# Cross-attention and routed FFN on one core: token list by two 128-column matmuls and a mask, down pieces a gap further up, third tile's logits by halves, first expert's pieces rearranged

## The chip, the core and the metric
The kernel runs on one core of a Trainium2 chip. A core has TensorE (PE), VectorE (DVE), ScalarE (ACT), GpSimd (POOL) and SyncE (SP), each with its own instruction queue, and they meet through semaphores. The metric is the device time of one execution in microseconds (us), as a median of several runs. The kernel before took 310.98 us (median of 3 runs, 310.86 to 312.36).

## The reference, cut to what matters
```python
# x: (2,1024,256)  ctx: (2,64,256)  16 heads of 64
def xattn(q_in, kv):                       # q_in = layernorm(x)
    q = einsum('bqc,chd->bqhd', q_in, Wq) / 8;  k, v = kv @ Wk, kv @ Wv
    a = einsum('bqhd,bkhd->bhqk', q, k)
    a = softmax(einsum('bhqk,hi->biqk', a, Wth1))      # heads mixed before
    a = einsum('bhqk,hi->biqk', a, Wth2)               # ... and after
    return einsum('bqhd,hdc->bqc', einsum('bhqk,bkhd->bqhd', a, v), Wo)
x = x + xattn(layernorm(x), ctx)
f = layernorm(x).reshape(2048, 256)
scores = (layer_norm(f) * g + b) @ centroids.T         # (2048, 8)
taken = all False
for e in range(8):                                     # balanced: 256 tokens each
    idx_e = top_k(where(taken, -inf, scores[:, e]), 256); taken[idx_e] = True
for e in range(8):
    h = layer_norm(f[idx_e]) * g + b
    out[idx_e] = f[idx_e] + gelu(h @ w1[e] + b1[e]) @ w2[e] + b2[e]
x = x + out
```

## The kernel before
**Attention.** The 2048 tokens are 16 tiles of 128. The head mixing is folded into two factors per batch: Am, which makes a tile's 1024 logits (16 heads by 64 keys) from its 256 columns of x, and Bm, which makes the tile's output from its 1024 probabilities. The tiles run through steps: in step s, tile s gets its logits, tile s-1 its exponential (ACT) and sums (DVE), tile s-2 is transposed on PE and multiplied with Bm, tile s-3 has its residual and layer norm, tile s-4 its scores and its row, which is stored to memory for the gathers of the experts. PE's function `attn` is in this order: first the 8 transposes of tile s-2, then 12 logits matmuls of tile s. An operand of a product in fp32r comes in two parts, a rounded one and a rest, and a product takes three matmuls (rounded with rounded, rounded with rest, rest with rounded, `mm3`). The statistics of x (`x_stats`, 16 tiles, `x_variance`, and POOL's `x_root`) are made by DVE early, tiles 8 to 15 in its loop over the factors' pieces.

**Routing.** For each of the 8 experts, DVE and PE find the 256th largest score by a search of 8 rounds of 4 bits. A round is `compare` (DVE, `cmpb` L1018), `total(k,r)` (PE, `oh_b,cntb`), the turn (DVE, `ok` L1035 and three small ones) and `narrow` (L1052). `select` and `ranks` follow: DVE makes `GE` and the running sums `INC`, PE multiplies them (`GE,tri_b` and `INC,ones_b`), and from this DVE gets each token's rank, marks the tokens as taken in `M`, and PE writes the next expert's scores with them (`cst,M`, `spread_scores`).

**Token list.** From each token's slot DVE makes one-hot tiles of its low and high half, `Loh` and `Hoh` (16 tiles by 16), POOL makes `Htk` = Hoh times token number, PE's `tokens` adds 16 products of 16 by 16 in PSUM, ACT's `lists_out` copies it to `Rt`, PE's `spread` multiplies with `exp_r` to spread it over 128 partitions, and DVE's `indices` picks by a mask and adds (`Rx`, `idx`). `idx` drives POOL's gather of the rows `G`.

**Experts.** An expert's rows are transposed (PE `cst,G`), scaled by ACT into `yF` (plain) and `yT` (rounded part), and POOL's `y_rest` makes the rest of yT. `up(e,f)`, f = 0..7, is six matmuls `yT,w1p` of 256 columns; ACT makes the gelu `hT`; `down(e,n)`, n = 0..15, is one fp32 matmul `w2s,hT`, two records in the trace. The last two experts have their down part as fp32r (`w2p,hp`), for which DVE's `hidden_split` makes two parts (`hp`, L1140 and L1142). DVE's `final` (L1059) adds the down result to the rows and POOL scatters them to the output.

**Order.** Slot k searches for expert k, makes the list of expert u = k-1, and does the up rest and the down part of expert e = k-2. Where PE's pieces stand is set by tables: `UP_FIRST`, `UP_REST`, `UP_LATE` and `DOWN` give, for each gap, which pieces run there; gap r is ahead of total(k,r), gap 8 between the last total and `ranks`, gap 9 behind `ranks`. All engines work through their queues in order. Through slot 1 there is no expert work ready, and PE runs products of `ones_b` (`keep_busy`) as padding. `lists_out` of expert 7's list and its `tokens` stand at the end of slot 7.

## Time and profile before
| what | value |
| --- | --- |
| median of 3 runs | 310.98 us (310.86 to 312.36) |
| profiled execution | 311.05 us |
| its span, first to last instruction | 309.3 us |
| granted TensorE clock, mean | 0.991 |
| busy: PE, DVE, ACT, POOL | 94%, 74%, 49%, 64% |
| instructions | 6795 |

The profiled execution took 1.75 us beyond its span. The stretches of the kernel in that trace: 0 to 50 us loads and factors, with the first logits; 50 to 164 the tiles, 7.14 us each (from the second to the third period: 72.09, 79.23, 86.37); 164 to 184 the search of slots 0 and 1, a round in 1.19 us; 184 to 297 the slots 2 to 8, the full ones in 15.3 us each; then the end of the last expert. In the rows below, a line of a timeline is the start in us, the duration in us, the engine, line, operation and tiles, with how many instructions it joins (x6), and in brackets the idle time of the engine just before and what ended it.

### The profile page before, as it was taken

To read this page: it belongs to the slowest core of one execution; us is meant where nothing else is said; L and a number is where in the kernel's file an instruction comes from. 1 tells how busy PE (TensorE), PEld (TensorE's weight loads), DVE (VectorE), ACT (ScalarE), POOL (GpSimd) and SP (SyncE) were. 2 spreads that over 40 slices of the span, in tenths; PEclk is the share of its full clock that TensorE was granted. 3 is DMA by queue.
4 is the path that set the end of the run, shared out by engine and by line. 5 is a ranking of instruction groups with operands and counts; after the bars stand their busy time and mean duration, and the time that the engine had idled before them with its cause. 6 is when DMAs were issued, how large, how long until landed. Compare 5 with 4: busy or idle time off the path is not lost.

```text
span 309.3 us, 6795 instructions
## 1 busy us (share of the span) xinstructions
PE 291.3 (94%) x2151; PEld 252.6 (82%) x2151; DVE 229.2 (74%) x799; ACT 151.0 (49%) x275; POOL 198.8 (64%) x248
## 2 busy tenths in 40 slices
PE   7999998999999999999987779999999999999990
PEld 3989997999999999999982239797989898989980
DVE  0569999888887888888877877777777777338750
ACT  1257646355555555554546424544444454564720
POOL 8200333467888888877742785949787878768841
PEclk9999999999999999999999999999999999999996
DMA  7995002971000000000116420555656565712120
GB/s 254 359 368 207 3 0 76 368 271 35 36 34 34 34 34 34 34 34 35 37 67 206 135 70 2 157 187 166 214 170 208 175 206 174 222 37 69 36 74 28
DMA packets 21769, 37.79 MB, mean 122 GB/s; under 512 B 2416, under 2 KB 14960, under 8 KB 21360
## 3 DMA queue, kind: packets, MB, share of 16 engines
q1 hardware_dynamic: 19184, 31.16, 29.4%
q0 software_dynamic: 2560, 6.31, 6.7%
q8 instruction: 14, 0.23, 0.3%
q14 instruction: 11, 0.09, 0.1%
HBM read 31.17 MB, written 6.29 MB: 121 GB/s over the span
## 4 chain that ended last, share of the span: by engine, by line
PE 77%; DVE 11%; issue 3%; POOL 3%; DMA 2%; ACT 1%; POOLq 0%; DVEq 0%
PE pair L1208 68%; PE pair L1284 4%; PE pair L1258 2%; DVE cmpb L1018 2%; PE pair L1452 1%; PE pair L1296 1%; DMA G<-rows_scratch,idx 1%; DMA out_dram<-G,idx 1%; DVE sm L875 1%; DVE wneg L789 1%; DVE pair L1052 1%; DVE hp L1140 1%; POOL out_dram L543 1%; DVE ok L1035 1%; POOL pr L284 0%
## 5 line engine op out<-in xcount | busy, mean ns | idle before, releaser
L1208 PE MATMUL pair<-yT,w1p 128*128 128x256 f32 x384 | 53.3, 290 | 0.0
L1208 PE MATMUL pair<-Bm,pT 128*128 (+1 forms) x384 | 50.4, 287 | 0.2 <-ACT pT L630 0.2
L1208 PEld LDWEIGHTS pair<-yT,w1p 128*128 128x128 f32 x384 | 48.2, 191 | 0.5 <-POOL yT L528 0.2
L1208 PE MATMUL pair<-Am,xTp 128*128 (+1 forms) x192 | 48.3, 400 | 0.0
L1208 PEld LDWEIGHTS pair<-Bm,pT 128*128 128x128 f32 x384 | 47.1, 191 | 0.4 <-issue 0.4
L1208 PE MATMUL pair<-w2s,hT 128*128 128x256 f32 x192 | 47.1, 389 | 0.0
L284 POOL TENSOR_TENSOR pr<-pr,rs 128x1024 f32<-128x1024 f32 (+1 forms) x16 | 31.3, 1955 | 24.3 <-DVE rs L882 15.2
L522 POOL TENSOR_TENSOR w1p<-w1s,w1p 128x512 fp32r<-128x512 f32 x32 | 40.1, 1280 | 5.7 <-ACT w1p L696 5.6
L1208 PEld LDWEIGHTS pair<-Am,xTp 128*128 128x128 f32 x192 | 34.9, 188 | 6.9
L1208 PEld LDWEIGHTS pair<-w2s,hT 128*128 128x128 f32 x192 | 33.8, 190 | 4.3
L741 ACT ACTIVATE hT<-pair,b1s 128x256 f32<-128x256 f32 x48 | 20.2, 471 | 34.4 <-PE pair L1208 20.9
L465 POOL TENSOR_TENSOR xTp<-xTs,xTp 128x256 fp32r<-128x256 f32 x16 | 11.9, 743 | 29.5 <-ACT xTp L597 29.5
L625 ACT ACTIVATE pr<-pr,r 128x1024 f32<-128x1024 f32 x16 | 18.4, 1149 | 25.2 <-DVE pr L927 25.2
L512 POOL DMA_INDIRECT G<-rows_scratch,idx x16 | 15.8, 987 | 17.3 <-DVE idx L1122 14.9
L1018 DVE TENSOR_SCALAR_CACHE_REDUCE cmpb<-pair 128x256 bf16<-128x256 f32 x48 | 23.5, 489 | 1.9
L923 DVE TENSOR_REDUCE mx<-pair 128x16 f32<-128x1024 f32 x16 | 19.5, 1221 | 4.1 <-PE pair L1208 3.9
L888 DVE TENSOR_TENSOR pT<-pair,pT 128x512 fp32r<-128x512 f32 x32 | 21.3, 668 | 0.3 <-ACT pT L630 0.3
L1208 PE MATMUL pair<-ones_b 128*128 128x512 bf16 x66 | 19.9, 424 | 1.5 <-DVE ones_b L778 1.5
L543 POOL DMA_INDIRECT out_dram<-G,idx x16 | 15.9, 992 | 7.7 <-DVE G L1059 3.1
L927 DVE TENSOR_TENSOR pr<-pair,mx 128x1024 f32<-128x1024 f32 x16 | 19.6, 1225 | 1.5
L1035 DVE SCALAR_TENSOR_TENSOR ok<-pair,cst 128x16 f32<-128x16 f32 x54 | 9.3, 173 | 13.8 <-PE pair L1208 13.7
L875 DVE TENSOR_REDUCE sm<-pr 128x16 f32<-128x1024 f32 x16 | 19.3, 1204 | 0.1
(156 smaller groups left out, 573.6 us busy)
## 6 DMA issues: line engine op xcount, KB each, us to landing
w1s<-w_dram SPq DMA_DIRECT2D x8, 1024.0 KB
w2s<-w_dram SPq DMA_DIRECT2D x7, 1024.0 KB, 5.8
rows_scratch<-row SPq DMA_DIRECT2D x16, 256.0 KB, 2.0
xs<-x_dram SPq DMA_DIRECT2D x1, 2048.0 KB, 16.7
xTs<-xT_dram SPq DMA_DIRECT2D x1, 2048.0 KB, 18.4
wk_s<-wk_dram SPq DMA_DIRECT2D x1, 1024.0 KB, 5.5
wv_s<-wv_dram SPq DMA_DIRECT2D x1, 1024.0 KB, 7.6
wqT_s<-wqT_dram SPq DMA_DIRECT2D x2, 512.0 KB, 9.2
```

The lines of the kernel that those rows point to most:

```text
L284: return eng.tensor_tensor(p4, p4, rs[:, v, :].unsqueeze(1).unsqueeze(3).to_broadcast([P, end - first, H, K8]), ALU.mult)
L512: pool.indirect_dma_start(out=G[:, b, a, :], out_offset=None, in_=rows_dram, in_offset=bass.IndirectOffsetOnAxis(ap=idx[:, e, a:a + 1], ax ...
L522: nc.gpsimd.tensor_tensor(w1p[:, 1, v, c, half], w1s[:, v, c, half], w1p[:, 0, v, c, half].bitcast(f32), ALU.subtract).then_inc(e_w1l, 1)
L543: pool.indirect_dma_start(out=out, out_offset=bass.IndirectOffsetOnAxis(ap=idx[:, e, a:a + 1], axis=0), in_=G[:, b, a, C:], in_offset=None ...
L625: nc.scalar.activation(pr[:, v, :], pr[:, v, :], ACT.Exp, scale=r1[:, ds(t, 1)]).then_inc(s_exp, 1)
L741: nc.scalar.activation(to, bank[1 + g % 2][:, h * CAP:(h + 1) * CAP], ACT.Gelu_apprx_tanh, bias=b1s[:, e * FC + f:e * FC + f + 1]).then_in ...
L875: nc.vector.tensor_reduce(sm[:, v, :], pr[:, v, :].rearrange("p (g i k) -> p i g k", g=KG, i=H), AX.XY, ALU.add).then_inc(s_sum, 1)
L888: nc.vector.tensor_tensor(pT[:, 1, v, q], probs_bank(t, g)[:], pT[:, 0, v, q].bitcast(f32), ALU.subtract).then_inc(s_pTs, 1)
L923: nc.vector.tensor_reduce(mx[:, v, :], pair[v][:].rearrange("p (g i k) -> p i g k", i=H, k=K8), AX.XY, ALU.max).then_inc(s_mx, 1)
L927: nc.vector.tensor_tensor(pr[:, v, :].rearrange("p (g i k) -> p g i k", i=H, k=K8), pair[v][:].rearrange("p (g i k) -> p g i k", i=H, k=K8 ...
L1018: nc.vector.tensor_scalar(cmpb[:], search_bank(k)[:, 0:T2 * P], thr.bitcast(f32), 0.0, ALU.is_ge, ALU.add, accum_out=cntb[:]).then_inc(r_c ...
L1208: return nc.tensor.matmul(out_, l, r, start=start, stop=stop)
```

## The change
It has six parts.

1. The list. `tokens` is two matmuls of 128 columns: the weights are 8 tiles of Loh, the moving operand 8 tiles of Htk, and of the 128x128 result only the blocks of a tile with itself count. DVE's new `lists_out` multiplies it with a mask `same_tile` into `Rt` (128x128), in place of ACT's 16x16 copy. `spread` takes all 128 rows and 128 columns, and `indices` multiplies 128x128 and reduces it to 2 columns. The mask lengthens the constants by 128 columns. `lists_out` stands ahead of compare(1,1) in slot 1 and behind compare and turn of round 1 in the other slots.
2. `DOWN[2]`: one down(n) of expert e goes from gap 8 to gap 2, and the others move up.
3. In step 2, the six logits matmuls of the first half of tile 2 go ahead of the transposes of tile 0. x_stats 8 to 15 go to DVE's steps 2, 3 and 4, and `x_root(1)` to POOL's step 5.
4. First expert: up(0,0) is split into a rounded part, ahead of total(1,7), and a rest; up(0,2) likewise behind it; up(0,1) behind `ranks`, up(0,3) behind `spread_scores`; the list of slot 2 stands between later ups, and two downs go to gap 2.
5. ACT writes yT, yT, yF, yF where it wrote yF, yT, yF, yT. Of the first expert's rows, DVE's `first_rows_rest` makes the second half's rest in the place of POOL, between narrow(1,7) and `select`.
6. In the last slot, `final(6,1)` stands ahead of hidden_split(7,2) and (7,3), not in round 2.

```diff
@@ token list
-        exp_r = sb("exp_r", [LO, P], f32r)
+        exp_r = sb("exp_r", [P, P], f32r)
-        Rt = sb("Rt", [LO, LO], f32r)
-        Rx = sb("Rx", [P, LO])
+        Rt = sb("Rt", [P, P], f32r)
+        Rx = sb("Rx", [P, LT, LO])
             def tokens(k):
...
-                for t in range(T):
-                    last = mm(bank[3][0:LO, 0:LO], Loh[:, t, :], Htk[:, t, :], t == 0, t == T - 1)
+                for h in range(T // LT):
+                    own = slice(h * LT, (h + 1) * LT)
+                    last = mm(bank[3][:, L_SUM:L_SUM + P], Loh[:, own, :].rearrange("p t n -> p (t n)"),
+                              Htk[:, own, :].rearrange("p t n -> p (t n)"), h == 0, h == T // LT - 1)
             def spread(k):
...
-                mm(bank[3][:, 32:32 + LO], exp_r[:], Rt[:], True, True).then_inc(r_Rx, 1)
+                mm(bank[3][:, L_OUT:L_OUT + P], exp_r[:], Rt[:], True, True).then_inc(r_Rx, 1)
-            def lists_out(u):                                   # ACT
-                act.wait_ge(r_R, u + 1)
-                nc.scalar.activation(Rt[:], bank[3][0:LO, 0:LO], ACT.Copy).then_inc(r_Rt, 1)
+            def lists_out(k):                                   # DVE
+                dve.wait_ge(r_R, k + 1)
+                nc.vector.tensor_tensor(Rt[:], bank[3][:, L_SUM:L_SUM + P], same_tile, ALU.mult).then_inc(r_Rt, 1)
             def indices(k):
...
-                nc.vector.tensor_tensor(Rx[:], bank[3][:, 32:32 + LO], smask, ALU.mult).then_inc(r_Rxm, 1)
+                nc.vector.tensor_tensor(Rx[:], bank[3][:, L_OUT:L_OUT + P].rearrange("p (t h) -> p t h", t=LT),
+                                        smask.unsqueeze(1).to_broadcast([P, LT, LO]), ALU.mult).then_inc(r_Rxm, 1)
@@ DVE's slot
+                    if k == 1 and r == 1:
+                        lists_out(u)
                     if counted:
                         compare(k, r)
                         if r > 0:
                             turn(k, r)
+                    if k > 1 and r == 1 and u < E - 1:
+                        lists_out(u)
...
+                    if r == 0 and k - 2 == E - 1:
+                        final(k - 3, 1)
                     if r == 0 and PARTED <= k - 2 < E:
                         hidden_split(k - 2, 2)
                         hidden_split(k - 2, 3)
-                    if r == 2 and 0 <= k - 3 < E:
+                    if r == 2 and 0 <= k - 3 < E and k - 2 != E - 1:
                         final(k - 3, 1)
...
+                if u == 0:
+                    first_rows_rest()
@@ attention
-                if isinstance(s, int) and s in (-1, 0):
-                    x_root(s + 1)
+                if isinstance(s, int) and s in (-1, 5):
+                    x_root(0 if s < 0 else 1)
+                    for n in {2: (8, 9), 3: (10, 11, 12), 4: (13, 14, 15)}.get(s, ()):
+                        x_stats(n)
+                    if s == 4:
+                        x_variance(1)
             def attn(s, u):
+                ahead = isinstance(s, int) and s == 2
+                if ahead:
...
+                    logits(s, par(s, u, 0), 0)
@@ rows
-                for c in range(CC):
-                    for to in (yF[:, c, :], yT[:, 0, v, c, :]):
-                        nc.scalar.activation(to, bank[0][:, c * CAP:(c + 1) * CAP], ACT.Identity,
+                for to in (yT[:, 0, v], yF):
+                    for c in range(CC):
+                        nc.scalar.activation(to[:, c, :], bank[0][:, c * CAP:(c + 1) * CAP], ACT.Identity,
+            def first_rows_rest():
+                c = CC - 1
+                dve.wait_ge(e_yT, CC + c + 1)
+                nc.vector.tensor_tensor(yT[:, 1, 0, c, :], yF[:, c, :], yT[:, 0, 0, c, :].bitcast(f32),
+                                        ALU.subtract).then_inc(e_yD, 1)
@@ tables
-            DOWN = {2: {3: (0, 3), 4: (3, 6), 5: (6, 8), 6: (8, 10), 7: (10, 13), 8: (13, 16)},
+            DOWN = {2: {2: (0, 1), 3: (1, 4), 4: (4, 7), 5: (7, 9), 6: (9, 11), 7: (11, 14), 8: (14, 16)},
@@ PE's slot
+                    if u == 0 and r == 7:
+                        up_rounded(u, 0)
...
-                        keep_busy(1 if k == 1 and r == 0 else BUSY)
+                        keep_busy({(1, 0): 1, (1, 6): 1, (1, 7): 0}.get((k, r), BUSY))
...
                 expert_part(k, 8)
+                if u == 0:
+                    up_rounded(u, 2)
+                    up_rest(u, 0)
+                    up_rest(u, 2)
...
                 expert_part(k, 9)
+                if u == 0:
+                    up(u, 1)
...
                     spread_scores(k + 1)
...
+                    if u == 0:
+                        up(u, 3)
```

PE's queue around the third tile, before. pair2<-cst,pr are the transposes of tile 0, Am,xTp the logits, of tile 2 here:
```order
L1208 MATMUL pair2<-ABT,mix 128x256 x4
L1208 MATMUL pair3<-ABT,mix 128x256 x4
L1284 MATMUL pair2<-cst,pr 128x128 x8
L1208 MATMUL pair0<-Am,xTp 128x512 x12
L1208 MATMUL pair3<-gcen0,inv_c 128x8 x2
```
The same place in the changed kernel:
```order
L1233 MATMUL pair2<-ABT,mix 128x256 x4
L1233 MATMUL pair3<-ABT,mix 128x256 x4
L1233 MATMUL pair0<-Am,xTp 128x512 x6
L1309 MATMUL pair2<-cst,pr 128x128 x8
L1233 MATMUL pair0<-Am,xTp 128x512 x6
L1233 MATMUL pair3<-gcen0,inv_c 128x8 x2
```
Six of the twelve logits matmuls have gone ahead of the eight transposes.

PE's queue from total(1,6) to total(2,2), where the first expert begins, before (oh_b,cntb is a total, yT,w1p an up, w2s,hT a down, Htk,Loh the tokens):
```order
L1208 MATMUL pair3<-oh_b,cntb 128x16
L1208 MATMUL pair0<-ones_b 128x512 x3
L1208 MATMUL pair0<-yT,w1p 128x256 x6
L1208 MATMUL pair3<-GE,tri_b 128x32
L1208 MATMUL pair3<-INC,ones_b 128x32
L1208 MATMUL pair0<-yT,w1p 128x256 x6
L1413 MATMUL pair3<-cst,M 128x128 x2
L1208 MATMUL pair1<-yT,w1p 128x256 x12
L1208 MATMUL pair3<-oh_b,cntb 128x16
L1208 MATMUL pair0<-yT,w1p 128x256 x6
L1208 MATMUL pair1<-Htk,Loh 16x16 x16
L1208 MATMUL pair0<-yT,w1p 128x256 x6
```
The same place after, from the padding behind total(1,6) on:
```order
L1233 MATMUL pair0<-yT,w1p 128x256 x4
L1233 MATMUL pair3<-oh_b,cntb 128x16
L1233 MATMUL pair1<-yT,w1p 128x256 x4
L1233 MATMUL pair0<-yT,w1p 128x256 x2
L1233 MATMUL pair1<-yT,w1p 128x256 x2
L1233 MATMUL pair3<-GE,tri_b 128x32
L1233 MATMUL pair3<-INC,ones_b 128x32
L1233 MATMUL pair0<-yT,w1p 128x256 x6
L1449 MATMUL pair3<-cst,M 128x128 x2
L1233 MATMUL pair1<-yT,w1p 128x256 x6
L1233 MATMUL pair0<-yT,w1p 128x256 x6
L1233 MATMUL pair3<-oh_b,cntb 128x16
```
Twelve ups' worth of matmuls stand ahead of the ranks where six stood, and up(0,4) has gone ahead of total(2,0); behind the last row come tokens, up(0,5), spread, up(0,6), total(2,1), up(0,7) and two downs.

DVE's queue in round 1 of slot 2, after (cmpb is the compare, Rt the new lists_out, Rx and idx the indices, each a row of its own in both kernels except Rt, which ACT did before):
```order
L1019 TENSOR_SCALAR cmpb,cntb<-pair3 128x256
L1029 TENSOR_TENSOR pair3<-pair3,ics 128x1
L1121 TENSOR_TENSOR Rt<-pair1,cst 128x128
L1126 TENSOR_TENSOR Rx<-pair1,cst 128x128
L1130 TENSOR_REDUCE idx<-Rx 128x2
L1036 SCALAR_TENSOR_TENSOR ok,acc<-pair3,cst 128x16
```
Between the turn and Rx there is one more instruction, and Rx is 128 wide where it was 16.

## Rows read from the trace of the kernel before
**Rows 1.** The page, part 1: busy time of each engine.
```profile
PE 291.3 (94%) x2151; PEld 252.6 (82%) x2151; DVE 229.2 (74%) x799; ACT 151.0 (49%) x275; POOL 198.8 (64%) x248
```
**Rows 2.** The page, part 4: the chain that ended last, by engine.
```profile
PE 77%; DVE 11%; issue 3%; POOL 3%; DMA 2%; ACT 1%; POOLq 0%; DVEq 0%
```
**Rows 3.** Waits of PE: releaser, us in total, times, longest.
```profile
PE pair L1208 <- DVE cmpb L1018: 4.7, 13, 0.6
```
**Rows 4.** Timeline, 49 to 54 us, the third tile.
```profile
50.40 0.86 PEld L1284 LDWEIGHTS pair<-cst,pr 128*128 128x128 f32 x8 [1.31 <-DVE Bm L783]
50.41 1.09 PE L1284 MATMUL pair<-cst,pr 128*128 128x128 f32 x8 [0.91 <-DVE Bm L783]
51.25 3.01 PE L1208 MATMUL pair<-Am,xTp 128*128 128x512 f32 x12
```
**Rows 5.** Timeline, 203.8 to 207.9 us, a list in slot 3.
```profile
203.87 0.18 PE L1208 MATMUL pair<-oh_b,cntb 128*128 128x16 bf16 x1
204.71 0.56 PE L1208 MATMUL pair<-Htk,Loh 128*16 128x16 f32 x16
204.90 0.49 DVE L1018 TENSOR_SCALAR_CACHE_REDUCE cmpb<-pair 128x256 bf16<-128x256 f32 x1
205.13 0.95 PE L1208 MATMUL pair<-yT,w1p 128*128 128x256 f32 x6
206.21 0.18 PE L1208 MATMUL pair<-oh_b,cntb 128*128 128x16 bf16 x1
206.25 1.67 PE L1208 MATMUL pair<-yT,w1p 128*128 128x256 f32 x12
207.84 0.18 PE L1208 MATMUL pair<-oh_b,cntb 128*128 128x16 bf16 x1
```
**Rows 6.** Timeline of PE (first row); lines by form: count, busy us, mean ns.
```profile
29.79 3.74 PE L1208 MATMUL pair<-mix,ABT 128*128 128x128 f32 x32
L825 DVE TENSOR_TENSOR mix<-wrep,cst 128x128 f32<-128x128 f32 x2 | 0.5, 283 | 0.0
L1122 DVE TENSOR_REDUCE idx<-Rx 128x2 int32<-128x16 f32 x8 | 1.4, 170 | 0.3
L875 DVE TENSOR_REDUCE sm<-pr 128x16 f32<-128x1024 f32 x16 | 19.3, 1204 | 0.1
L799 DVE BATCH_NORM_STATS2 bst<-xs 128x6 f32<-128x256 f32 x16 | 6.7, 420 | 0.0
```
**Rows 7.** Timeline, 176 to 186 us, slot 1.
```profile
176.66 0.17 DVE L1119 TENSOR_TENSOR Rx<-pair,cst 128x16 f32<-128x16 f32 x1
184.16 0.18 PE L1208 MATMUL pair<-oh_b,cntb 128*128 128x16 bf16 x1 [0.35 <-DVE cmpb L1018]
185.89 0.18 PE L1208 MATMUL pair<-INC,ones_b 128*128 128x32 bf16 x1
```
**Rows 8.** Timeline, 199.2 to 200.7 us, gap 8 of slot 2.
```profile
199.24 1.54 PE L1208 MATMUL pair<-w2s,hT 128*128 128x256 f32 x6
200.13 0.22 DVE L1075 TENSOR_TENSOR_SCAN INC<-pair,GE 128x32 bf16<-128x32 f32 x1
```
**Rows 9.** Timeline, total(2,2).
```profile
192.54 0.18 PE L1208 MATMUL pair<-oh_b,cntb 128*128 128x16 bf16 x1
```
**Rows 10.** Line L1150: shortest, median, longest in ns, and when.
```profile
L1150 DVE TENSOR_TENSOR yT<-yF,yT x2: 412/988/1564, 286.8 to 288.3; 128x256 fp32r<-128x256 f32 x2
```
**Rows 11.** Timeline, the lists of slots 7 and 8.
```profile
264.89 0.64 POOL L501 TENSOR_TENSOR Htk<-Hoh,cst 128x256 fp32r<-128x256 f32 x1
265.58 0.57 PE L1208 MATMUL pair<-Htk,Loh 128*16 128x16 f32 x16
...
274.95 0.75 PE L1208 MATMUL pair<-Htk,Loh 128*16 128x16 f32 x16
```
**Rows 12.** Timeline of POOL, 185.5 us.
```profile
185.53 1.43 POOL L536 TENSOR_TENSOR G<-G,b2s 128x256 f32<-128x256 f32 x2
```
**Rows 13.** Timeline, 297 us.
```profile
297.81 3.80 PE L1208 MATMUL pair<-w2p,hp 128*128 128x256 f32 x30 [0.57 <-DVE G L1059]
```

More of the change, by code:

```diff
@@ L35 @@
 LO = 16
+LT = P // LO
 EPS = 1e-5
@@ L525, in y_rest @@
             def y_rest(e, v):
-                for c in range(CC):
-                    pool.wait_ge(e_yT, 4 * e + 2 * c + 2)
+                for c in range(CC if e > 0 else 1):
+                    pool.wait_ge(e_yT, 4 * e + CC + c + 1)
                     nc.gpsimd.tensor_tensor(yT[:, 1, v, c, :], yF[:, c, :], yT[:, 0, v, c, :].bitcast(f32),
@@ L656, in attn @@
                 if live(t):
-                    if isinstance(s, int) and s in (1, 4):
+                    if isinstance(s, int) and s in (1, 6):
                         act.wait_ge(s_r1, 1 if s == 1 else 2)
@@ L752, in _ @@
                     hidden(e, e % 2, g)
-                if 0 <= u < E - 1:
-                    lists_out(u)
                 for g in rest[1:]:
@@ L766, in _ @@
                     if u == E - 2:
-                        lists_out(E - 1)
                         w2_part(E - 1, 0)
@@ L833, in _ @@
                     x_variance(0)
-                if MIXED <= f < MIXED + T // 2:
-                    x_stats(T // 2 + f - MIXED)
-            x_variance(1)
             def x1_add(t, v):
@@ L1195, in _ @@
                 if u == E - 2:
+                    lists_out(E - 1)
                     w2_rest(E - 1, 0)
@@ L1321, in attn_rest, with logits @@
                 last.then_inc(s_pv, 1)
-            def attn(s, u):
+            def logits(t, v, g):
+                for c in range(CC):
+                    last = mm3(bank[2 * v + g][:], lambda i: xTp[:, i, v, c * P:(c + 1) * P],
+                               lambda i: Am[:, i, ds(t // (T // B), 1), c, g * 512:(g + 1) * 512].rearrange(
+                                   "p b n -> p (b n)"), c == 0, c == CC - 1)
+                if g == 1:
+                    last.then_inc(s_lg, 1)
+            def attn(s, u):
+                ahead = isinstance(s, int) and s == 2
+                if ahead:
+                    pe.wait_ge(s_xTs, s + 1)
+                    pe.wait_ge(s_sub, s - 1)
+                    logits(s, par(s, u, 0), 0)
                 t = s - 2
@@ L1341, in attn @@
                     wait(pe, s_sub, t - 1)
-                    for g in range(2):
-                        for c in range(CC):
-                            last = mm3(bank[2 * v + g][:], lambda i: xTp[:, i, v, c * P:(c + 1) * P],
-                                       lambda i: Am[:, i, ds(t // (T // B), 1), c, g * 512:(g + 1) * 512].rearrange(
-                                           "p b n -> p (b n)"), c == 0, c == CC - 1)
-                    last.then_inc(s_lg, 1)
+                    for g in range(1 if ahead else 0, 2):
+                        logits(t, v, g)
                 for f in late(s):
@@ L1454, in rows, with up_bank, up_free @@
                 last.then_inc(e_gT, 1)
-            def up(e, f):
-                v, g, q = e % 2, f // 2, f % 2
-                if f == 0:
-                    pe.wait_ge(e_w1l, W1_PARTS * (e + 1))
-                if q == 0:
+            def up_bank(f):
+                return bank[1 + f // 2 % 2][:, f % 2 * CAP:(f % 2 + 1) * CAP]
+            def up_free(e, f):
+                g = f // 2
+                if f % 2 == 0:
                     if g >= 2:
@@ L1522, in expert_part @@
                 if 0 <= e < E:
-                    for f in range(*UP_REST[first_part(e)].get(gap, (0, 0))):
+                    rest, downs = (UP_REST[first_part(e)], DOWN[first_part(e)]) if e > 0 else (UP_REST_0, DOWN_0)
+                    for f in range(*rest.get(gap, (0, 0))):
+                        if e == 0:
+                            list_of_tokens(k, gap, 1 - f % 2)
                         up(e, f)
-                        list_of_tokens(k, gap, f % 2)
-                    for n in range(*DOWN[first_part(e)].get(gap, (0, 0))):
+                        if e > 0:
+                            list_of_tokens(k, gap, f % 2)
+                    for n in range(*downs.get(gap, (0, 0))):
                         down(e, n)
                 u = k - 1
-                if 0 <= u < E:
-                    first = UP_LATE if 0 < u < SPLIT else UP_FIRST[first_part(u)]
+                if 0 < u < E:
+                    first = UP_FIRST[4] if u >= SPLIT else UP_LATE if u > 1 else UP_LATE_1
                     for f in range(*first.get(gap, (0, 0))):
```

66 lines of the change are left out of this document (42 added, 24 removed).

## The prediction
> **What bounds the kernel now.** I read the page first: TensorE is busy 94% of the span [rows 1], at a mean granted clock of 0.991, and the chain of waits lies on it for 77%, on VectorE for 11% [rows 2]. So a change is worth what it takes from TensorE's queue, or from the few places where TensorE waits. Three of its waits bear on the change: 4.7 us on the search's comparison, 13 times, all in the first slots [rows 3], .91 us once on the copy of Bm, which ends at 50.41 ahead of tile 0's transposes [rows 4], and .57 us once on the final add L1059, which ends at 297.81 [rows 13]. The comparisons lie between 164 and 184 us, where VectorE's chain is the bound, a round takes about 1.19 us and TensorE pads with ones_b. Behind total(1,7) at 184.16 [rows 7] TensorE is full again to 297 us, in slots of 15.3 us.
>
> **Prices from rows.** 12 "up" matmuls between two totals take 1.59 us: 206.25 to 207.84 [rows 5], .133 each, so one `up` of six is .80. Three down(n), six records, take 1.38, from 199.24 to 200.62 [rows 8]: .46 each. A list costs TensorE the stretch from total(0) 203.87 to total(1) 206.21 [rows 5], 2.34 us, less two `up` (1.59): .75 us. Of it the 16 narrow `tokens` are .42 (204.71 to 205.13) and the rest is `spread` with its turn-round.
> A 128-column fp32r matmul is in no row. From below: eight 128-column transposes in .86 us of weight loads [rows 4], .107 each. From above: the two passes of a plain fp32 matmul of that width, 32 records in 3.74 us [rows 6], .234 for a pair. I take .107, because all other fp32r matmuls here go in one pass like the transposes. VectorE's 128x128 with two operands is .283 [rows 6], against .17 for Rx now [rows 7]; the reduction over 128 lies between the .170 of 16 columns and the 1.204 of 1024 [rows 6], in proportion .29.
>
> **1. Third tile.** TensorE now stands from 49.50 to 50.41 [rows 4]. With six logits matmuls (1.5 us, half of 3.01) ahead of the transposes they fill the gap and transposes start at 51.0, when Bm is copied far enough; the rest follows without a gap: **−.91**. The moved x_stats (eight of .42 [rows 6]) and x_variance run in VectorE's slack of about 1 us in each tile of 7.14, over three tiles; GpSimd's x_root is needed a tile later. I cost them at 0. If that cover were missing, one tile's exponential would start .4 to .9 us later and the whole gain would go. The longer constants (64 KB more) end well before their first use: 0.
>
> **2. List and search in slot 1.** Here VectorE is the bound. `lists_out` (.29, start to start .21) goes ahead of compare(1,1), and Rx and idx grow by .12 each; not all of it shows, since Rx and idx partly lie in the wait for total(1) [rows 7]: **+.32** on total(1,7), bounds 0 and .53. TensorE's pieces of `up` on both sides of total(1,7) take the place of padding. Then comes `first_rows_rest` (.41 by its twin [rows 10]) in VectorE's queue between narrow and select. ScalarE makes both rounded copies first, so the plain ones end near 185.0; GpSimd does its half until about 185.4; VectorE's piece follows, and GE, INC come near 186.3. INC on TensorE, 185.89 now [rows 7], comes near **186.5**. From there TensorE has up(0,1), the scores' pair, up(0,3), up(0,4): .80+.26+.80+.80, total(2,0) at 189.17. VectorE in slot 2 needs, as after 203.87 in rows 5, 1.03 to compare(1), .41 to the end of its turn and .41 for the mask: Rt at 191.0; TensorE has tokens .21 and up5 .80 and waits **.8** at `spread`. Then spread .13, up6, up7 and two downs (.93): total(2,2) at 193.71. Before it was at 192.54 [rows 9] with those two downs (.93) still to do, 193.47. So **+.24**, with the wider index work **+.29** for the first expert. What is late next is `spread`: the mask is queued behind VectorE's compare and turn, and all of TensorE's ups stand behind `spread`.
>
> **3. Slots 3 to 6.** `tokens` .42 becomes .21, `spread` with its wait .33 becomes about .26: −.28 per list. The moved down costs .46 in gap 2 and leaves gap 8. There two downs end at 199.21+.95, but INC is ready at 200.35 on VectorE [rows 8], 1.18 behind total(7), so TensorE waits .21: it was at its ups at +1.46, now at +1.21. That is −.25 for .46 moved, +.21. Together **−.07** a slot, −.28 for four. Against it: GpSimd starts Htk behind bias and scatters, and TensorE now reaches `tokens` earlier, while ScalarE's new order (rounded, rounded, plain, plain) gives GpSimd its first piece .45 later. Slots 4 to 6 then wait about .08 each: +.25. Net **−.03**. What is queued behind that wait is up5, spread and total(1).
>
> **4. Slot 7.** Htk ends at 265.53 and `tokens` starts at 265.58 [rows 11]: no slack at all. The list is .28 cheaper and about .40 of GpSimd's delay comes out: **+.12**. **Slot 8**, list of the last expert: 274.95 to 275.56 [rows 11], .61 becomes .21, and its Htk has long been there: **−.40**.
>
> **5. Tail.** In the last slot final(6,1) goes ahead of the hidden_split pairs 2 and 3. Before, TensorE waited .57 until 297.81 for L1059 [rows 13], which stood in VectorE's queue behind the last L1142. Now L1059 is done earlier and the wait is for the hidden rest at 297.7: .10. **−.47**. GpSimd's scatter of that half goes earlier, with no one behind it; the end is still the last down, add and scatter.
>
> **Sum.** −.91 +.29 −.03 +.12 −.40 −.47 = −1.40 us, against the profiled execution's 311.05 (span 309.3 and 1.75 around it): **309.65**. That execution is .07 above the median of 310.98, so I say 309.6. The change is 0.45%; a difference under 0.5% (1.55 us) is about what a measurement here can't tell from none.
>
> **The port.** The row first: VectorE's yT<-yF,yT beside GpSimd's w1p took 1.56 us the first time and .41 the second [rows 10], mean .99; GpSimd's instruction beside it ended at 288.12. The Trainium skill ("SBUF — State Buffer", Who interferes with whom) says that a VectorE instruction with two SBUF inputs and a GpSimd one that reads SBUF exclude each other, the later one blocked until the other is through. The trace agrees, .41 against 1.56. By that rule `first_rows_rest` would wait out whatever GpSimd has just begun.
>
> **Rivals.**
> B, slower: the wide fp32r matmul runs at the price of two passes. Place: `tokens` and `spread` of every list; .234 for .107 three times is +.38, less .06 where the wait at `spread` takes it in: +.32 a list, seven lists +2.2: **311.9**. It decides from .2 us a matmul. For it: no row of this shape. Against it: the 256-column ones at .133.
> C, no gain: VectorE's new subtraction loses to GpSimd. After its half GpSimd goes straight to two bias adds of 1.43 [rows 12]; if the first one of these gets in, VectorE waits to about 187.0, INC and all behind it come 1.4 us later: **311.0**. For it: the 1.56 us row. Against it: VectorE's piece would be queued already while GpSimd's y_rest runs, and the row has it run as soon as one GpSimd instruction ends.
> D, more gain: wide matmuls nearer .07, no waits for Htk in slots 4 to 7 (−.65), `spread` in slot 2 waits less: **308.6**.
> The skill has a price for this: "TensorE: Matmul & The Clock Gate", Back-to-back issue gap, gives about 81 ns for a 128-column matmul in a stream of loads and matmuls; by an estimate from that figure, three of them a list are .08 less than by .107, and the sum would be 309.0 to 309.1. The trace's nearest row has 107 ns.
> E: the reordering does nothing for TensorE at the third tile because VectorE or ScalarE fall behind with tile 2: −.91 goes, 310.5.
>
> **Numbers.** Forecast .45 (its own range 309.0 to 310.3), D .20, C with E .20, B .12, anything else .03. The range of 8 in 10 reaches from D to B's middle: 308.4 to 311.9. Faster by over 0.5% (below 309.43): D and two fifths of the forecast, plus a little of the rest: .40. Slower by over 0.5% (above 312.5): B at its worst with C's wait on top: .10. Within: .50.
>
> **What would show it.** In the profile after: no wait on Bm near 49.5, and tile periods still 7.14 us; PE tokens as two records about .1 apart; total(1,7) near 183.6 (184.16 −.91 +.32), INC near 185.6; a wait of TensorE on VectorE's Rt at slot 2 of about .8 and in no later slot; a wait of about .2 on INC in gap 8 of slots 2 to 6; waits on GpSimd's Htk in slots 4 to 7; the last wait below .2. Wrong would be: `first_rows_rest` longer than 1 us (C), wide matmuls above .2 (B), a wait between 50 and 72 us on VectorE or ScalarE (E), or no wait on Htk (D).

## The result and the profile after
The changed kernel took **307.88 us** (median of 4 runs, 307.38 to 308.50) against 311.65 (4 runs, the three of the recorded 310.98 and one more): ratio 0.9886, 95% interval 0.9857 to 0.9915. The forecast was 309.6, its range 308.4 to 311.9: the direction was right, the size too small, and the time lies below the range. The same kernel, timed again later beside other kernels, took 309.05 (7 runs), ratio 0.9929 (0.9905 to 0.9954); experiment 6 shows what differs. The profiled execution took 308.50, its span was 306.7, the mean granted clock 0.992 (before 0.991).

The page after, parts 1 and 4, against [rows 1, 2]:
```profile
PE 287.6 (94%) x2034; PEld 249.2 (81%) x2034; DVE 233.1 (76%) x808; ACT 148.7 (48%) x267; POOL 197.5 (64%) x247
PE 77%; DVE 8%; POOL 5%; DMA 4%; issue 3%; ACT 1%; SPq 0%; POOLq 0%; DVEq 0%
```
The waits of TensorE after, against [rows 3]:
```profile
PE pair L1233 <- DVE cmpb L1019: 4.7, 12, 0.9
PE pair L1233 <- DMA wk_s<-wk_dram: 1.4, 1, 1.4
PE pair L1233 <- DVE Rt L1121: 0.6, 2, 0.5
PE pair L1233 <- POOL Htk L505: 0.3, 1, 0.3
```
The waits on Bm and on the last add are gone; Rt and Htk are new. The 1.4 us on the first weights' DMA is no part of the change: `pad` below, which does the work of the kernel before, has 1.2, and the first logits come between 36.32 (`oldlist`) and 38.97 us (`after2`) in traces of kernels that do the same up to there.

Timeline of TensorE after, the third tile, against [rows 4]:
```profile
49.77 1.74 PE L1233 MATMUL pair<-Am,xTp 128*128 128x512 f32 x6
51.34 1.04 PE L1309 MATMUL pair<-cst,pr 128*128 128x128 f32 x8
52.13 1.63 PE L1233 MATMUL pair<-Am,xTp 128*128 128x512 f32 x6
```
A list in slot 3 after, against [rows 5]:
```profile
203.22 0.18 PE L1233 MATMUL pair<-oh_b,cntb 128*128 128x16 bf16 x1
204.05 0.34 PE L1233 MATMUL pair<-Htk,Loh 128*128 128x128 f32 x2
204.22 0.92 PE L1233 MATMUL pair<-yT,w1p 128*128 128x256 f32 x6
205.06 0.33 PE L1233 MATMUL pair<-Rt,exp_r 128*128 128x128 f32 x1
205.23 0.18 PE L1233 MATMUL pair<-oh_b,cntb 128*128 128x16 bf16 x1
206.79 0.59 PE L1233 MATMUL pair<-w2s,hT 128*128 128x256 f32 x2
207.22 0.17 PE L1233 MATMUL pair<-oh_b,cntb 128*128 128x16 bf16 x1
```
`tokens` takes .17 (204.05 to 204.22) where it took .42, and total(k,0) to total(k,1) 2.01 where it took 2.34. The stretch with the new down, total(k,1) to total(k,2), is gap 2 and takes 1.99 where it took 1.63. Slot 3 as a whole takes 15.31, no less than before; slot 4 takes 15.09 (total(4,0), total(4,1), total(4,2)):
```profile
218.52 0.18 PE L1233 MATMUL pair<-oh_b,cntb 128*128 128x16 bf16 x1
220.54 0.18 PE L1233 MATMUL pair<-oh_b,cntb 128*128 128x16 bf16 x1
222.52 0.17 PE L1233 MATMUL pair<-oh_b,cntb 128*128 128x16 bf16 x1
```
Slots 1 and 2 after (GpSimd's and VectorE's half of the first rest, INC; then Rt and `spread` of slot 2), against [rows 7, 10]:
```profile
183.67 0.73 POOL L532 TENSOR_TENSOR yT<-yF,yT 128x256 fp32r<-128x256 f32 x1 [0.78 <-ACT yF L713]
184.08 0.60 DVE L1157 TENSOR_TENSOR yT<-yF,yT 128x256 fp32r<-128x256 f32 x1
185.24 0.18 PE L1233 MATMUL pair<-INC,ones_b 128*128 128x32 bf16 x1
189.49 0.28 DVE L1121 TENSOR_TENSOR Rt<-pair,cst 128x128 fp32r<-128x128 f32 x1
189.82 0.33 PE L1233 MATMUL pair<-Rt,exp_r 128*128 128x128 f32 x1 [0.47 <-DVE Rt L1121]
```
VectorE's piece starts while GpSimd's runs (until 184.40) and ends .28 behind it, as the one of 1.56 us [rows 10] ended .28 behind GpSimd's. The end, against [rows 13]:
```profile
292.94 6.10 PE L1233 MATMUL pair<-w2p,hp 128*128 128x256 f32 x48
299.08 0.42 DVE L1060 TENSOR_TENSOR G<-pair,G 128x256 f32<-128x256 f32 x1 [2.05 <-PE pair L1233]
```
48 matmuls in one stretch, with no wait between the first 18 and the last 30.

**Where the 2.6 us of span went**, from the starts of the same matmuls in both traces:

| stretch | before | after | change | forecast |
| --- | --- | --- | --- | --- |
| start to the first logits | 36.63 | 37.17 | +.54 | 0 |
| to the logits of tile 3 | 22.03 | 20.96 | -1.07 | -.91 |
| to total(1,0); tile period 7.140, now 7.113 | 116.45 | 116.10 | -.35 | 0 |
| to total(3,0), first expert | 28.76 | 28.99 | +.23 | +.29 |
| to INC of slot 6 | 57.98 | 57.27 | -.71 | -.03 |
| to `spread` of the last list | 16.60 | 16.22 | -.38 | -.28 |
| to the end of the span | 30.80 | 29.97 | -.83 | -.47 |

Without the start's +.54 the change gave 3.1 us, of which 1.4 were forecast. The 1.7 between them are .68 in slots 3 to 6, .36 at the end, .35 in the tiles, .16 at the third tile, .10 in the last two lists and .06 at the first expert.

### The profile page after: what moved, and what is told of

Its sections match the earlier page's. It is cut to its first block, busy times and chain, and to the rows that moved or that the text cites. A ratio compares the mean times of both kernels' runs of the same rounds, so it can differ in the third digit from the quotient of the medians.

```text
span 306.7 us, 6418 instructions
## 1 busy us (share of the span) xinstructions
PE 287.6 (94%) x2034; PEld 249.2 (81%) x2034; DVE 233.1 (76%) x808; ACT 148.7 (48%) x267; POOL 197.5 (64%) x247
## 4 chain that ended last, share of the span: by engine, by line
PE 77%; DVE 8%; POOL 5%; DMA 4%; issue 3%; ACT 1%; SPq 0%; POOLq 0%; DVEq 0%
PE pair L1233 67%; PE pair L1309 4%; PE pair L1283 2%; DMA wk_s<-wk_dram 2%; DVE cmpb L1019 1%; POOL w2p L556 1%; PE pair L1491 1%; DMA G<-rows_scratch,idx 1%; PE pair L1321 1%; POOL G L516 1%; DMA out_dram<-G,idx 1%; DVE wneg L787 1%; POOL out_dram L547 1%; POOL yT L532 1%; PE pair L1449 1%
## 5 line engine op out<-in xcount | busy, mean ns | idle before, releaser
L1233 PE MATMUL pair<-Bm,pT 128*128 128x256 f32 (+1 forms) x384 | 49.9, 285 | 0.2 <-ACT pT L634 0.2
L1233 PE MATMUL pair<-Am,xTp 128*128 128x512 f32 (+1 forms) x192 | 48.9, 402 | 0.0
L713 ACT ACTIVATE yT<-pair,gbs 128x256 fp32r<-128x256 f32 x16 | 8.2, 559 | 23.8 <-PE pair L1491 23.8
L1233 PE MATMUL pair<-ones_b 128*128 128x512 bf16 x61 | 17.9, 413 | 1.5 <-DVE ones_b L776 1.5
```

What stands on the lines that cost most here:

```text
L1233: return nc.tensor.matmul(out_, l, r, start=start, stop=stop)
```

## The experiments
All ratios are to the kernel before, timed on the same chip. The names in the quoted expectations are these kernels'. "Slot" is total(k,0) to total(k+1,0).

**1. The list and the moved down, each without the other.** The theory: VectorE bounds gap 2 once the list is wide, and the down lies in its shadow. The rival: each has its own price. `olddown` and `downonly` differ from the changed kernel and from the kernel before in the one line:
```diff
-            DOWN = {2: {2: (0, 1), 3: (1, 4), 4: (4, 7), 5: (7, 9), 6: (9, 11), 7: (11, 14), 8: (14, 16)},
+            DOWN = {2: {3: (0, 3), 4: (3, 6), 5: (6, 8), 6: (8, 10), 7: (10, 13), 8: (13, 16)},
```
(`downonly` has it the other way round). `oldlist` has the whole of part 1 undone but for the longer constants:
```diff
-                for h in range(T // LT):
...
+                for t in range(T):
+                    last = mm(bank[3][0:LO, 0:LO], Loh[:, t, :], Htk[:, t, :], t == 0, t == T - 1)
```


> The changed kernel with the table DOWN[2] as before (three downs each in gaps 3, 4, 7 and 8, none in gap 2; the first expert keeps its own table). Theory 1 (with the wide list VectorE needs about .2 us more between total(1) and total(2), and the down in gap 2 fills that): total(k,1) to total(k,2) is near 1.83 and not 1.63 in slots 3 to 6, total(k,7) to INC 1.44, the slot 15.18 where it is 15.08, in all +.4 us. Theory 2 (the down costs its .35 us wherever it stands): total(k,1) to total(k,2) is 1.63, the slot is 14.98, in all -.4 us. Theory 3, my forecast's step (.46 for a down, .25 back): -.2 a slot against gap 8 +.25, within .2 of no change.

> The changed kernel with the token list as before: tokens as 16 matmuls of 16 columns, ScalarE copies 16x16 to Rt, spread and indices narrow. All other parts stay changed, the longer constants too. Theory 1 (the wide list is worth its 128-column matmuls at about .1 us each and costs VectorE about .2 more between total(1) and total(2)): total(k,0) to total(k,1) goes from 2.01 back to 2.34 us in slots 3 to 6, total(k,1) to total(k,2) stays 1.98 or falls by under .1, the wait at spread in slot 2 (.47) goes, slot 1 is .3 shorter. In all 1.0 to 1.6 us longer than the changed kernel. Theory 2 (the gain in the slots comes from the moved down, not from the list): 2.01 stays within .1 of 2.1, less than .6 us in all.

> The kernel before with only the table DOWN[2] of the changed kernel: a down moved from gap 8 to gap 2, for the first expert as for the next ones; the list stays narrow and on ScalarE. Theory 1 (the moved down pays only beside the wide list, whose VectorE work makes gap 2 last 1.95 us anyway): gap 2 goes from 1.63 to 1.98, gap 3 from 1.47 to 1.41, gap 8 from 1.44 to 1.20, the next stretch from 3.22 to 3.27, a slot of 15.30 becomes 15.40, in all +.4 to +.5 us. Theory 2 (the moved down is the part that pays, .2 us a slot): 15.1, in all -1.0 us.

| kernel | list | gap 2 | gap 3 | gap 8 | slot | us, ratio |
| --- | --- | --- | --- | --- | --- | --- |
| before (slot 5) | 2.34 | 1.63 | 1.47 | 1.44 | 15.30 | |
| olddown (slot 4) | 2.02 | 1.95 | 1.47 | 1.44 | 15.28 | 308.85, 0.9895 (0.9854 to 0.9936) |
| downonly (slots 3, 5) | 2.35 | 1.99 | 1.41 | 1.20 | 15.43 | 311.39, 1.0000 (0.9984 to 1.0016) |
| oldlist (slots 3 to 5) | 2.34 to 2.45 | 1.99 | 1.40 | 1.19 | 15.4 to 15.55 | 309.88, 0.9949 (0.9931 to 0.9967) |
| changed (slots 4, 5) | 2.02 | 1.98 | 1.41 | 1.20 | 15.08 | 307.88, 0.9886 |

Gap 8 is total(k,7) to INC. The wide list alone gives .02 a slot, the moved down alone costs .13, both together give .22. These are differences within traces; the time of `downonly` (ratio 1.0000 within .0016) can't tell its .13 a slot from none. Timeline of VectorE and TensorE in `olddown`, gap 2 of slot 4:
```profile
220.23 0.19 PE L1233 MATMUL pair<-oh_b,cntb 128*128 128x16 bf16 x1
220.43 0.29 DVE L1126 TENSOR_TENSOR Rx<-pair,cst 128x128 f32<-128x128 f32 x1 [0.42 <-PE pair L1233]
220.75 0.29 DVE L1130 TENSOR_REDUCE idx<-Rx 128x2 int32<-128x128 f32 x1
220.96 0.16 DVE L1036 SCALAR_TENSOR_TENSOR ok<-pair,cst 128x16 f32<-128x16 f32 x1
221.62 0.49 DVE L1019 TENSOR_SCALAR_CACHE_REDUCE cmpb<-pair 128x256 bf16<-128x256 f32 x1
222.18 0.18 PE L1233 MATMUL pair<-oh_b,cntb 128*128 128x16 bf16 x1 [0.24 <-DVE cmpb L1019]
```
Rx and idx now hold ok back to .73 behind its total (.40 before), the comparison follows, and TensorE waits .24. With a down there instead of the wait, gap 2 is 1.98: .03 more. In `downonly` TensorE takes 1.99 there with no wait, total(2,1) to total(2,2):
```profile
206.13 0.18 PE L1208 MATMUL pair<-oh_b,cntb 128*128 128x16 bf16 x1
208.12 0.17 PE L1208 MATMUL pair<-oh_b,cntb 128*128 128x16 bf16 x1
```
In `olddown` the comparison starts .56 ahead of total(k,2) (221.62 to 222.18). In the kernel before it is .56 too, with no wait of TensorE, so VectorE was already level with it there (against total(3,2) at 207.84 [rows 5]):
```profile
207.28 0.49 DVE L1018 TENSOR_SCALAR_CACHE_REDUCE cmpb<-pair 128x256 bf16<-128x256 f32 x1
```
Theory 1 of olddown had the sign and the mechanism (slot +.20, forecast there +.10; gap 2 at 1.95, forecast 1.83). The whole of `oldlist` is 2.0 us slower than the changed kernel, more than expected: its lists in slots 4 to 6 take 2.44 to 2.48, because `tokens` comes .08 to .12 later there, right behind a late Htk, and its tile period is 7.140 again (experiment 3).

**2. The third tile.** `oldthird`: TensorE's old order, all else changed.
```diff
-                ahead = isinstance(s, int) and s == 2
+                ahead = False
```


> The changed kernel with TensorE's order at the third tile as before: the eight transposes of tile 0 ahead of all twelve logits matmuls of tile 2; the statistics of x stay moved. Theory 1 (the order alone fills a hole of TensorE that is 1.1 us long, though the matmul row shows .91 of idle): TensorE stands again near 50 us, the fourth tile starts 1.1 us later than in the changed kernel, in all +1.1. Theory 2 (the order gives the .91 of the idle row and the rest of the 1.1 is the moved statistics): +.9. Theory 3 (VectorE's freed time gives most of it): +.5 or less.

308.98 us, 0.9918 (0.9881 to 0.9955): 1.10 more than the changed kernel. First logits to those of tile 3: 22.05, against 20.96 and 22.03 before. All of the 1.07 is the order, and the moved statistics cost nothing. The timeline shows the wait again:
```profile
50.23 1.09 PE L1309 MATMUL pair<-cst,pr 128*128 128x128 f32 x8 [0.87 <-DVE Bm L781]
```

**3. The tile period.** `pad` and `pad2` do the work of the kernel before, with tiles made longer:
```diff
-C_W, C_OH, C_END = 0, 128, 256, 264, 280, 296, 312, 440, 568, 584
+C_W, C_OH, C_END = 0, 128, 256, 264, 280, 296, 312, 440, 568, 712
...
-        Rt = sb("Rt", [LO, LO], f32r)
-        Rx = sb("Rx", [P, LO])
+        Rt = sb("Rt", [P, P], f32r)[0:LO, 0:LO]
+        Rx = sb("Rx", [P, P])[:, 0:LO]
```
(`pad` has only the first.)

> The kernel before, with nothing changed but the constants' tile made 128 columns longer (712, filled with zeros), so that everything behind it in SBUF lies 512 bytes further on. Theory 1 (the tile period fell from 7.14 to 7.11 us because the operands lie elsewhere): the period is 7.11 here and the kernel .3 us shorter than the one before. Theory 2 (the period depends on something else, as the two traces being of different executions): 7.14, no difference.

> The kernel before, with the constants' tile 128 columns longer and the tiles Rt and Rx made 128 columns wide, of which the old 16 are used: the layout in SBUF of the changed kernel with the work of the kernel before. Theory 1 (the tile period of 7.113 us in the changed kernel and 7.138 before is a matter of where tiles behind Rt and Rx lie): 7.113 here, in all -.3 us. Theory 2 (the period follows something in the instructions): 7.138.

`pad`: 311.09 us, 0.9997 (0.9972 to 1.0022), period 7.140. `pad2`: 310.67 us, 0.9979 (0.9958 to 1.0000), period 7.113. Two tiles of each, `pad2` first:
```profile
79.89 3.02 PE L1208 MATMUL pair<-Am,xTp 128*128 x12
87.00 3.02 PE L1208 MATMUL pair<-Am,xTp 128*128 x12
```
```profile
79.96 3.02 PE L1208 MATMUL pair<-Am,xTp 128*128 x12
87.10 3.02 PE L1208 MATMUL pair<-Am,xTp 128*128 x12
```
From the logits of tile 3 to total(1,0), `pad2` takes 116.09, the kernel before 116.45. The .35 us is the place of tiles in SBUF, not work: with the longer constants alone it does not come, with Rt and Rx wider too it does. Which tile gains was not tried.

**4. The first expert's parts.** `oldfirst` has TensorE's pieces of part 4 as before; `poolrest` has both halves of the rest on GpSimd; `actorder` has ScalarE's four copies as before:
```diff
-                    if u == 0 and r == 7:
-                        up_rounded(u, 0)
...
```
```diff
-                if u == 0:
-                    first_rows_rest()
```
```diff
-                for to in (yT[:, 0, v], yF):
-                    for c in range(CC):
+                for c in range(CC):
+                    for to in (yF, yT[:, 0, v]):
```


> The changed kernel with TensorE's order for the first expert as before: padding in slot 1, up(0,0) behind total(1,7), up(0,1) behind ranks, no extra up ahead of total(2,0), one down in gap 2 of slot 2 as in the later slots; VectorE still makes the second half's rest. Theory 1 (the rearranged pieces hid little, for total(3,0) of the changed kernel came .22 us late against the search of slot 1): slot 2 takes 15.1 where it takes 15.24 and total(2,0) comes at most .1 later, in all 0 to .3 us shorter than the changed kernel. Theory 2 (the pieces that replace padding are worth the .5 to .8 us of TensorE work that they take from slot 2): .4 to .8 us longer.

> The changed kernel with both halves of the first expert's rest on GpSimd, as before; nothing stands on VectorE between narrow(1,7) and select. Theory 1 (VectorE's piece costs .52 us between narrow and GE, and TensorE, which waits for GpSimd's first half until 184.7, has no need of the second much earlier): INC can come .5 earlier but TensorE waits for GpSimd's second half, ready some .7 later than VectorE's; INC at +1.9 to +2.1 behind total(1,7) where it is +1.68, in all +.2 to +.4. Theory 2 (VectorE's piece is the price): INC at +1.3, in all -.3.

> The changed kernel with ScalarE's order of the rows' four copies as before (plain, rounded, plain, rounded). Theory 1 (the new order serves the first expert's rounded matmuls and costs GpSimd .4 us of lead in every later slot): Htk starts .4 earlier against total(k,0) in slots 4 to 6 (-.4 where it is 0 to +.23), no wait of TensorE on Htk in slot 7, but up_rounded(0,0) comes later and INC of slot 1 at +1.8 to +2.0 where it is +1.68; in all between -.3 and +.1. Theory 2 (the order is worth its place): INC of slot 1 at +2.2 or later, +.4 us or more.

From total(1,0) to total(3,0) (before 28.76, changed 28.99): `oldfirst` **28.85**, slot 2 15.12, so theory 1: as they stand, the rearranged pieces cost .1 in slot 2. The whole stretch says .14, but it varies: seven traces of kernels that are the same there have 28.99 to 29.23. `poolrest` 29.43, INC at +2.11 behind total(1,7) (changed +1.68, in the other six traces +1.70 to +1.71): theory 1, VectorE's piece is worth .4. `actorder` 31.14: TensorE waits 1.0 for ScalarE's rounded copies ahead of total(1,7), which comes 1.07 later, INC comes at +2.11, and slot 1 is 2.16 longer in all. That is theory 2, though INC stayed under its +2.2 and the loss was over its .4. The times (308.64, 309.37, 310.09; ratios 0.9914, 0.9930, 0.9955) hold the effect of experiment 6 too, so only the stretches are compared.

**5. The tail.** `oldfinal` has the add in round 2 again:
```diff
-                    if r == 0 and k - 2 == E - 1:
-                        final(k - 3, 1)
```


> The changed kernel with final(6,1) in round 2 of the last slot as before, behind all hidden_split pieces. Theory 1 (the add was what TensorE's last 30 matmuls waited for): TensorE waits .57 near 295 us on L1060, in all +.5. Theory 2 (the wait would have been taken by the last hidden_split in any case): under +.2.

309.65 us, 0.9937 (0.9918 to 0.9957). The wait is back, .56 until 296.49, as theory 1 had it. But the kernel is 1.8 slower than the first set of the changed kernel, not .5 (against the second set, below, .6).

**6. The late ok, and a faster version.** Slots 4 to 6 of `oldfinal` show the rest: lists of 2.27, 2.50 and 2.44. `rthtk` had shown the same, where it was to take two waits away:
```diff
-                    if k == 1 and r == 1:
+                    if k in (1, 2) and r == 1:
                         lists_out(u)
...
-                    scatter(k - 3)
+                    scatter(k - 3, (0,))
+                    if k == E - 2:
+                        token_rows(k)
+                    scatter(k - 3, (1,))
```


> The changed kernel with two waits of TensorE taken away: in slot 2 lists_out stands ahead of compare(2,1), as in slot 1, and in slot 7 GpSimd makes Htk ahead of the second scatter, not behind it. Theory 1 (both waits are TensorE's own loss, .47 us on Rt and .28 on Htk): total(2,0) to total(2,1) falls from 2.79 to about 2.4, INC of slot 6 to tokens from 4.18 to 3.8, in all -.6 to -.8 against the changed kernel. Theory 2 (VectorE's comparison, now later, takes the place of Rt in slot 2, and the scatter's delay hits a gather or the rest of w1 in slot 7): within .2 of the changed kernel.

307.99 us, 0.9885 (0.9847 to 0.9923). Slot 2 fell from 15.24 to 14.61 and the wait for Htk in slot 7 went (INC to `tokens` 3.73), but slots 4 and 5 took .23 and .61 more (.17 of that a gather): no gain in sum. `best` does the same in slots 3 to 6 (`if 3 <= k < E - 1`), `htkall` does that without the edit of slot 2, `oldfinalhtk` on top of `oldfinal`.

> The changed kernel with lists_out ahead of compare(2,1) in slot 2, and with GpSimd making Htk between the two scatters in slots 3 to 6 (for the lists of slots 4 to 7), where in rthtk it did so only for slot 7's. Theory 1 (in rthtk total(k,0) to total(k,1) grew from 2.02 to 2.25 and 2.45 in slots 4 and 5 because Htk ran on GpSimd just when VectorE wanted to read total(k,0)'s result, and the ok came .46 and .66 behind the total instead of .23): Htk a whole us earlier takes this away, 2.02 in all slots, slot 2 14.6, in all -.8 to -1.1 against the changed kernel. Theory 2 (the late ok has to do with the scatter or with GpSimd's w1 rest): 2.25 to 2.45 again somewhere, -.1 to -.4.

> The changed kernel again, word for word, for a time on the same chip as the runs beside it and a second trace. Theory 1 (whether VectorE's ok comes .23 or .45 to .7 behind total(k,0) in slots 4 to 6 is fixed by the kernel, as the times of the kernels with it, .5 to 1.2 us longer in every execution, say): .23 in slots 4 to 6 again, 307.9. Theory 2 (it is a matter of chance from execution to execution): .45 or more in some slot, and times that spread by 1 us.

> The changed kernel with GpSimd making Htk between the two scatters in slots 3 to 6; lists_out of slot 2 stays behind the comparison. Theory 1 (the late ok does not occur in the changed kernel, so all that this edit can give there is the wait on Htk in slots 5 to 7): -.3 to -.5 us against the changed kernel, slot 2 as before 15.24. Theory 2 (most of what the combined kernel gained came from Htk): -.7 or more.

> The kernel oldfinal (final(6,1) in round 2 of the last slot) with GpSimd's Htk between the two scatters in slots 3 to 6. In oldfinal total(k,0) to total(k,1) was 2.27, 2.50 and 2.44 in slots 4 to 6, and ok .48 to .71 behind the total. Theory 1 (that comes of Htk running on GpSimd while VectorE wants to start ok, and 1.15 us of oldfinal's loss are this and only .57 are the add): 2.02 in all slots, -1.4 to -1.6 against oldfinal, 308.0 to 308.3. Theory 2 (the late ok comes from elsewhere): 2.25 or more stays in some slot, less than -1 us.

`after2` is the changed kernel itself. Slot 5 in the first trace of it, then in `after2`, then in `best`: total, Htk, ok.
```profile
233.61 0.18 PE L1233 MATMUL pair<-oh_b,cntb 128*128 128x16 bf16 x1
233.82 0.64 POOL L505 TENSOR_TENSOR Htk<-Hoh,cst 128x256 fp32r<-128x256 f32 x1
233.84 0.17 DVE L1036 SCALAR_TENSOR_TENSOR ok<-pair,cst 128x16 f32<-128x16 f32 x1 [0.47 <-PE pair L1233]
```
```profile
235.78 0.18 PE L1233 MATMUL pair<-oh_b,cntb 128*128 128x16 bf16 x1
236.01 0.63 POOL L505 TENSOR_TENSOR Htk<-Hoh,cst 128x256 fp32r<-128x256 f32 x1
236.43 0.17 DVE L1036 SCALAR_TENSOR_TENSOR ok<-pair,cst 128x16 f32<-128x16 f32 x1 [0.88 <-PE pair L1233]
237.71 0.28 DVE L1121 TENSOR_TENSOR Rt<-pair,cst 128x128 fp32r<-128x128 f32 x1
238.04 0.33 PE L1233 MATMUL pair<-Rt,exp_r 128*128 128x128 f32 x1
```
```profile
231.73 0.61 POOL L505 TENSOR_TENSOR Htk<-Hoh,cst 128x256 fp32r<-128x256 f32 x1 [0.21 <-issue]
232.60 0.18 PE L1237 MATMUL pair<-oh_b,cntb 128*128 128x16 bf16 x1
232.84 0.17 DVE L1040 SCALAR_TENSOR_TENSOR ok<-pair,cst 128x16 f32<-128x16 f32 x1 [0.46 <-PE pair L1237]
```
Behind the same total, with Htk at the same place, ok starts .23 or .65 later. The delay passes through comparison and Rt to `spread`: total(5,0) to total(5,1) is 2.02 or 2.44. In `downonly`, where ScalarE still makes Rt, ok comes at .45 to .48 and the list stays at 2.34. In slot 4 of `rthtk`, where VectorE makes it, ok at .46 makes the list 2.25 for 2.02. The late ok costs something only since Rt stands behind it on VectorE.

| kernel | ok behind total, slots 4, 5, 6 | Htk against total | lists | us, ratio |
| --- | --- | --- | --- | --- |
| changed, first | .23 .23 .23 | 0 to +.23 | 2.02 | 307.88, 0.9886 |
| after2 | .50 .65 .66 | +.07 to +.23 | 2.29 2.44 2.45 | 309.05, 0.9929 |
| oldfinal | .48 .71 .65 | +.07 to +.27 | 2.27 2.50 2.44 | 309.65, 0.9937 |
| oldfinalhtk | .23 .23 .23 | -.88 | 2.02 | 308.48, 0.9903 (0.9867 to 0.9938) |
| htkall | .23 .23 .23 | -.88 | 2.02 | 307.69, 0.9877 (0.9844 to 0.9910) |
| best | .23 .24 .22 | -.87 | 2.02 | **307.07**, 0.9862 (0.9831 to 0.9892) |

Theory 1 of after2, that it belongs to the kernel, fell. The three lists of `after2` together are 1.12 longer than in the first trace, the median 1.17. Within one set of runs the executions agree, between sets they don't: 307.4 to 308.5 in the first, 308.6 to 309.8 in the second but for one of 311.46, whose trace has 1.9 us of DMA wait at its start. With Htk .9 us earlier the late ok was in none of three kernels: theory 1 of oldfinalhtk and of best hold, though oldfinalhtk gave -1.2 against oldfinal, not -1.4. `htkall` is .2 faster than the first set and 1.4 than the second. The median of `best` is .8 and 2.0 us below the two sets of the changed kernel. Against the first the intervals of the ratios overlap; there the trace decides, with total(1,0) to total(3,0) 28.47 where it was 28.99, and no wait for Htk in slot 7.

That Htk has to do with it is well supported. In fourteen of the seventeen traces Htk still runs when ok is due in slots 4 to 6, and nine of these have a late ok, which starts .37 to .52 behind Htk's own start (the kernel before and `pad2` among them, .32 to .35 behind the total). In the three with Htk already done ok is never late. But Htk is not enough: the other five (the first, `olddown`, `oldlist`, `oldthird`, `pad`) have .23 all the same, and in `rthtk` slot 5 has .66 and slot 6 .23 with Htk at +.25 and +.24. What decides between the two stays open: no run here tells it.

## Why the prediction was wrong
Point by point, in the order of its steps.

- **Bound by TensorE, few waits:** right; a change was worth what it took from TensorE's queue or from its waits. But in gap 2 VectorE's chain was already level with TensorE, and widening two small instructions made it the bound there.
- **1, third tile, -.91:** right mechanism, size 1.07, and 1.09 in `oldthird` against the changed kernel. The matmul row's idle starts at the modelled end of the last matmul; the weight loads' row, in the same group [rows 4], has 1.31. The moved statistics cost nothing, as forecast.
- **0 for the rest of attention:** missed .35; the layout, which no view of the trace before could show.
- **2, first expert, +.29:** measured +.23, by two errors that cancel, so the near hit is luck. total(1,7) came +.28 where +.32 was forecast. INC came at 185.24 where 186.5, less the .88 by which slot 1 started earlier, is 185.62: .12 of this is GpSimd's half, done at 184.40 and not 184.52, .13 is VectorE's piece, which took .28 behind it and not .41, .13 the way from there to INC. The wait at `spread` was .47 in the matmul row, not .8, but total(2,2) came 7.21 behind INC, as forecast. Then .37 was lost again in the rest of slot 2, and .27 of it I did not see: with one up less behind `ranks`, TensorE's weight load for the next scores stands waiting for M. Ahead of `ranks` there stand two ups (12 matmuls) where one stood.
- **3, slots 3 to 6, -.03: the step that failed.** "The moved down costs .46 in gap 2": in that gap the wide list has made VectorE the bound at 1.95, and the down costs .03 there; against the kernel before gap 2 and gap 3 together take .29 more. The list's own -.32 and gap 8's -.24 were as forecast (.28, .25). Slots 4 and 5 gave .22 each, not .07. That I priced Rx and idx in slot 1 and not in gap 2 of the slots is the error. The waits on Htk, priced at +.25 in all, moved `tokens` by .06 and .08 in slots 5 and 6 and cost nothing: those lists are 2.02 too, for `spread` then takes .06 where it took .17. So of the .68 that slots 3 to 6 were better than forecast, .25 is this term. Slot 3 lost its .22 to a narrow(3,7) that started .44 behind its ok and not .22:
```profile
213.26 1.41 POOL L532 TENSOR_TENSOR yT<-yF,yT 128x256 fp32r<-128x256 f32 x2 [0.97 <-ACT yF L713]
214.48 0.17 DVE L1053 TENSOR_TENSOR pair<-pair,acc 128x1 int32<-128x1 int32 x1 [0.25 <-DVE ok L1036]
```
What held it is not shown: GpSimd's y_rest runs beside it, but at the same place in slots 4 and 5 too, where it is not late. It is late in slot 3 of eleven of the thirteen traces with the changed order, and not in `oldlist` and `poolrest`.
- **4, slots 7 and 8, -.28:** -.38. The wait for Htk shows as .28 in slot 7:
```profile
264.67 0.44 PE L1233 MATMUL pair<-Htk,Loh 128*128 128x128 f32 x2 [0.28 <-POOL Htk L505]
```
INC to `tokens` is 4.18 where it was 3.73, +.45 for a forecast of about .40. The last list's `tokens` took .36 (274.02 to 274.38), so -.25 and not -.40; `spread` with nothing behind it to wait for took .06 where 16 columns had taken .20.
- **5, tail, -.47:** the wait of .57 went altogether; I had kept .10 for the hidden rest, which was in time. The other .26 is the last list's cheaper `spread` (.14) and small differences over 40 matmuls.
- **Rivals:** B is out, a 128-column fp32r matmul takes .085 (two in .17). C is out: VectorE's piece was done .28 behind the end of GpSimd's half, and it was GpSimd's two bias adds behind it that took longer, 1.61 where 1.43 [rows 12]. The Trainium skill's rule on this ("SBUF — State Buffer", Who interferes with whom) agrees: the piece took .60 where its twin alone took .41. D was nearest in number, 308.6 for 307.9, but not for its reasons: the waits for Htk that it had at nothing came, and its own terms (.65, and .037 three times in seven lists, .78) would have given 308.2. The Trainium skill ("TensorE: Matmul & The Clock Gate", Back-to-back issue gap) has about 81 ns for a 128-column matmul in a stream of loads and matmuls; the 85 measured here are nearer to that than my 107. E is out, the third tile gave its wait.

In sum: the direction and the third tile's mechanism were right, most of the miss is in the slots (the down's price and the waits on Htk), and the tiles' .35 was put at nothing.

The forecast's own range, 309.0 to 310.3, holds the second set (309.05). That is luck: that set is longer by the late ok, which the forecast did not have.
